# One norm for two and late-turned keys in a second attention's context, and one 96-row product for three in a third expert layer

## The reference

```python
x = x + jnp.tanh(g_xattn[1]) * _L1_xattn_ref(_layernorm(x, axis=-1), ctx_1024, ...)
x = x + jnp.tanh(g_ffn[2]) * _L2_ffn_ref(_layernorm(x, axis=-1), ...)

def _L1_xattn_ref(x, context, Wq, Wkv, Wo, null_kv, q_scale, k_scale, ...):   # 16 heads of 64
    xn = layer_norm(x, ln_in_g, ln_in_b)          # x comes in normalised already: two norms in a row
    cn = layer_norm(context, ln_ctx_g, ln_ctx_b)
    q = xn @ Wq
    k, v = jnp.split(cn @ Wkv, 2, axis=-1)
    ...                                           # a null key and value are appended
    q = l2_normalize(q) * q_scale
    k = l2_normalize(k) * k_scale
    ...

def _L2_ffn_ref(x, gate_W, gate_b, wi_W, wi_b, wo_W, wo_b, lora_A, lora_B):   # E = 8, R = 4, F = 1024
    logits = jnp.einsum('bsd,ed->bse', x, gate_W) + gate_b
    top1 = jnp.argmax(jax.nn.softmax(logits, axis=-1), axis=-1)
    base = jnp.einsum('bsd,fd->bsf', x, wi_W) + wi_b
    for i in range(lora_A.shape[0]):
        lora = jnp.einsum('bsr,fr->bsf', jnp.einsum('bsd,rd->bsr', x, lora_A[i]), lora_B[i])
        inter = jax.nn.relu(base + lora)
        expert_out = jnp.einsum('bsf,df->bsd', inter, wo_W) + wo_b
        out = out + (top1 == i)[..., None] * expert_out
```

## Time and profile before

| | us |
|---|---|
| median of 3 runs | 1950.33 |
| lowest and highest run | 1947.45, 1950.34 |
| profiled execution, whole | 1967.21 |
| profiled execution, span of its trace | 1965.4 |
| TensorE, VectorE, ScalarE, GpSimd busy in the span | 1740.6, 1260.9, 975.3, 529.6 |

### The profile page before, as it was taken

One profiled execution on the slowest core, in us unless ns is written; L12 is line 12 of the kernel. 1 busy time (PEld: TensorE's weight loads), 2 busy tenths in 40 slices (PEclk: granted clock), 3 DMA queues, 4 the chain that ended last, 5 costly groups with the idle time before them and its releaser, 6 DMA issues. The chain is left out here.

```text
span 1965.4 us, 32371 instructions
## 1 busy us (share of the span) xinstructions
PE 1740.6 (89%) x11712; PEld 1417.1 (72%) x11712; DVE 1260.9 (64%) x2310; ACT 975.3 (50%) x1739; POOL 529.6 (27%) x492
## 2 busy tenths in 40 slices
PE   6998799967799997599999969999799789798895
PEld 4666799922577776599999558888577566588884
DVE  6886688545255554688888657765534688666643
ACT  4652466413587763367776234443533255416740
POOL 2220343253323432222221540000200143313333
PEclk9998899978799998699999979999799899999998
DMA  3003478420100000666675230000000200026743
GB/s 112 17 18 98 165 250 255 131 64 0 49 1 7 12 12 25 207 216 237 232 236 203 76 117 1 1 1 1 23 1 1 59 6 17 28 84 207 233 131 94
DMA packets 97139, 178.32 MB, mean 91 GB/s; under 512 B 25184, under 2 KB 61946, under 8 KB 95914
## 3 DMA queue, kind: packets, MB, share of 16 engines
q1 hardware_dynamic: 85496, 146.00, 22.5%
q0 software_dynamic: 11232, 30.69, 5.3%
q10 hardware_dynamic: 288, 0.00, 0.0%
HBM read 149.38 MB, written 27.26 MB: 90 GB/s over the span
## 5 line engine op out<-in xcount | busy, mean ns | idle before, releaser
L1669 POOL DMA_INDIRECT f_block_rows_home<-normed_x,f_token_of_sb x138 | 168.6, 1222 | 425.5 <-PE psum L1715 325.4
L1695 PE MATMUL psum<-f_block_h_sb,f_w1h_home 128*128 128x256 f32 x736 | 211.4, 287 | 30.5 <-DVE f_block_l_sb L1889 11.9
L1695 PE MATMUL psum<-f_block_l_sb,f_w1h_home 128*128 128x256 f32 x736 | 207.0, 281 | 0.0
L1695 PE MATMUL psum<-f_block_h_sb,f_w1l_home 128*128 128x256 f32 x736 | 206.9, 281 | 0.0
L2321 PE MATMUL psum<-a_xT_home,context_w 128*128 128x256 f32 x704 | 181.7, 404 | 13.6 <-PEq L122 9.7
L1705 PE MATMUL psum<-f_w2h_home,f_hidden_h_home 128*128 128x256 f32 x644 | 187.4, 291 | 3.3 <-DVE f_result_sb L1600 2.4
L1705 PE MATMUL psum<-f_w2h_home,f_hidden_l_home 128*128 128x256 f32 x644 | 181.7, 282 | 0.0
L1705 PE MATMUL psum<-f_w2l_home,f_hidden_h_home 128*128 128x256 f32 x644 | 181.7, 282 | 0.0
L1695 PEld LDWEIGHTS psum<-f_block_h_sb,f_w1h_home 128*128 128x128 f32 x736 | 141.0, 192 | 38.5 <-issue 28.6
L2492 ACT ACTIVATE a_probsT_sb<-psum 77x1024 f32<-77x1024 f32 (+1 forms) x128 | 130.8, 1022 | 68.9 <-PE psum L2373 66.3
L2321 PEld LDWEIGHTS psum<-a_xT_home,context_w 128*128 128x128 f32 x704 | 132.1, 197 | 45.1 <-issue 20.0
(11 more groups left out here) (314 smaller groups left out, 3924.1 us busy)
## 6 DMA issues: line engine op xcount, KB each, us to landing
f_w_sb<-in_f_w SPq DMA_DIRECT2D x161, 512.0 KB
sorted_y<-f_result_sb SPq DMA_DIRECT2D x69, 256.0 KB
normed_x<-f_xn_all SPq DMA_DIRECT2D x24, 256.0 KB, 2.1
f_b_row_sb<-in_f_b SPq DMA_DIRECT2D x46, 128.0 KB
f_w_sb<-in_f_w SPq DMA_DIRECT2D x23, 256.0 KB
f_block_rows_home<-normed_x,f_token_of_sb POOLq DMA_INDIRECT x138, 4.3
residual<-in_x SPq DMA_DIRECT2D x8, 256.0 KB, 6.4
context_w<-in_a_wk SPq DMA_DIRECT2D x2, 1024.0 KB, 5.0
```

The lines of the kernel that those rows point to most:

```text
L1669: nc.gpsimd.indirect_dma_start(block_rows[b % 2][:, h, :], None, xs, bass.IndirectOffsetOnAxis(ap=column, axis=0)).then_inc(sems[f"rows_in ...
L1695: last = nc.tensor.matmul(hid_ps(q)[:, m, :], w, rhs, start=(j == 0), stop=(j == len(parts) - 1))
```

## The change

In the context of a1: the two norms in a row are one, with the variance v replaced by v (1 + e) + e^2 (e = 1e-5), so `normalise_once`, `variance_again`, `normalise_again` and the second power go. All 16 value products come first, through four banks; keys are projected one batch a round, and a batch's keys are turned two rounds later; two row tiles are normalised in each of VectorE's rounds and turned two rounds later, through two banks (2 and 3). In the end of f0, `COMBINED` is (5, 11) for (1, 7). In f2: the masked values are written three times beside each other, turned into 96 x 512, and rounded once in place; the second 32 rows then become the rest of u, and the factor `lb`, loaded three times below itself, is rounded, with its third 32 rows made the rest. So `u3` is (uh, ul, uh) and `lb3` is (lbh, lbh, lbl), and one 96-row product gives the three terms. TensorE does the 24 wide products of the first chunk ahead of the turns, and VectorE splits the first weights and inputs within the choice (`beside`).

```diff
@@ rows_part
-        nc.vector.tensor_scalar(var[:, tiles], mv[:, tiles, 1], EPS, None, ALU.add).then_inc(sems["var_done"], 1)
+        if own:
+            last = nc.vector.tensor_scalar(var[:, tiles], mv[:, tiles, 1], 1.0 + EPS, EPS * EPS, ALU.mult, ALU.add)
...
-    def normalise_once(dve, tiles):
-    def variance_again(dve, halves):
-    def normalise_again(dve, tiles):
...
@@ context_part
-    V_BANKS = 1 if own else 4
-    VALUES_FIRST = 10
-    v_bank = lambda j: psum[0:CTX, 6 if own else 4 + j % 4, 0:VN]
+    V_BANKS = 4
+    v_bank = lambda j: psum[0:CTX, (0 if own else 4) + j % 4, 0:VN]
-    key_banks = lambda b: slice(4 * (b % 2), 4 * (b % 2) + 2)
+    key_banks = lambda b: slice(4 + 2 * (b % 2), 6 + 2 * (b % 2))
...
-            if b == 2:
-                rows["power"](pool, 1, slice(0, TILES))
...
-        return range(2 * b - NBATCH, 2 * b - NBATCH + 2) if b >= NBATCH // 2 else range(0)
+        return range(b - 2, b - 1) if 2 <= b < NBATCH else range(NBATCH - 2, NBATCH) if b == NBATCH else range(0)
...
+        for j in range(len(v_list)):
+            value_products(pe, j)
+        for b in range(NBATCH + 2):
+            if b < NBATCH:
+                project(b)
+            for k in rows_beside(b):
+                rows["turn"](pe, k)
+            if b >= 2:
+                turn_keys(b - 2)
...
+        for j in range(len(v_list)):
             own_values_out(j)
+        for b in range(NBATCH + 2):
+            if b < NBATCH:
+                take(b)
+                squares(b)
             for k in rows_beside(b):
                 rows["turned_out"](act, k)
-            spread(b)
+            if b >= 2:
+                spread(b - 2)
...
+        for b in range(NBATCH + 1):
+            if b < NBATCH:
+                sum_squares(b)
+                rows["normalise"](dve, 0, b)
+            if b:
+                normalise_keys(b - 1)
...
@@ choose_low_rank
-        choose.softmax_rows(dve, step, choose.c)
+        choose.shift(dve, step)
+        t["beside"](dve)
+        choose.softmax_rest(dve, step, choose.c)
...
+        nc.vector.tensor_copy(um[:, :, 1:3, :], um[:, :, 0:1, :].to_broadcast([P, TILES, 2, 32])).then_inc(
+            sems["masked"], 1)
...
@@ experts
-        sp.dma_start(lb[:], dram[f"{name}_lb"]).then_inc(sems["lora_in"], 16)
+        for part in range(3):
+            sp.dma_start(lb[part * 32:(part + 1) * 32, :, :], dram[f"{name}_lb"]).then_inc(sems["lora_in"], 16)
...
+        def low_rank(u, c, m):
+            if m == 0 and u == 0:
+                pe.wait_ge(sems["lora_low"], 1)
+                pe.wait_ge(sems["u_low"], c + 1)
+            nc.tensor.matmul(hid_ps[m], lb3[:, u, m * P:(m + 1) * P], u3[:, chunk(c)], start=False,
+                             stop=True).then_inc(sems["hidden"], 1)
+
+        def begin():
+            for m in range(HC):
+                whole_rank(0, 0, m)
+            turn_inputs(0)
+            turn_inputs(1)
+            for m in range(HC):
+                low_rank(0, 0, m)
+            turn_inputs(2)
+            turn_inputs(3)
...
-            nc.scalar.activation(ust[:, k % 2, :], u_ps(k), ACT.Copy)
-            high(uh[:, chunk(k)], u_ps(k), "u_high")
+            high(u3[:, chunk(k)], u_ps(k), "u_high")
         high(w1h[0][:], w1raw[0][:], "w1_high")
+        high(xh[:, :, chunk(0)], xT[:, :, chunk(0)], "x_high")
         t["exponentials"](act)
...
-            low(ul[:, chunk(k)], ust[:, k % 2, :], uh[:, chunk(k)], "u_low")
+            low(u3[32:64, chunk(k)], u_ps(k)[32:64, :], u3[32:64, chunk(k)], "u_low")
...
         dve.wait_ge(sems["lora_high"], 1)
+        low(lb3[64:96], lb[64:96], lb3[64:96], "lora_low")
+        x_low(1)
+        weight_lows(0, 2)
         inputs_low(0)
...
@@ routed_experts
-    COMBINED = (1, 7) if shared == 1 else (4, 12, 20)
+    COMBINED = (5, 11) if shared == 1 else (4, 12, 20)
...
```

More of the change, by code:

```diff
@@ L258, in rows_part @@
     sems = {k: env["sem"](f"{name}r_{k}") for k in (
-        "loaded", "chain", "var_done", "rstd_done", "once", "stats2", "x_normed", "x_turned", "x_out")}
+        "loaded", "chain", "var_done", "rstd_done", "x_normed", "x_turned", "x_out")}
     ln_in = sb("ln_in", [P, 2, DC]) if own else None
@@ L572, in project, with turn_keys @@
             last.then_inc(sems["k_ready"], 1)
[L574 to L585, removed]
+        def turn_keys(b):
             pe.wait_ge(sems["k_normed"], b + 1)
@@ L650, in spread @@
                     keysT[:, part * 4:part * 4 + 4, b, :],
-                    psum[:, 2 + part, 0:4 * keys].rearrange("p (c k) -> p c k", k=keys), ACT.Copy, scale=k_scale[:])
+                    psum[:, part, 0:4 * keys].rearrange("p (c k) -> p c k", k=keys), ACT.Copy, scale=k_scale[:])
             last.then_inc(sems["kn_out"], 1)
[L654 to L657, removed]
+        for j in range(len(v_list)):
             own_values_out(j)
[L659 to L667, removed]
+        for b in range(NBATCH + 2):
+            if b < NBATCH:
+                take(b)
+                squares(b)
             for k in rows_beside(b):
                 rows["turned_out"](act, k)
-            spread(b)
+            if b >= 2:
+                spread(b - 2)
     def scalar(act):
@@ L727, in sum_squares, with normalise_keys @@
             nc.vector.tensor_scalar(ss[b % 3][:], ss[b % 3][:], 1e-24, None, ALU.max).then_inc(sems["squared"], 1)
-        sum_squares(0)
-        sum_squares(1)
-        for b in range(NBATCH):
+        def normalise_keys(b):
             dve.wait_ge(sems["inverted"], b + 1)
@@ L1275, in experts, with run_ahead @@
     y_ps = [psum[:, 4 + q, 0:D] for q in range(4)]
-    u_ps = lambda k: psum[0:32, 4 + k % 2, :]
+    u_ps = lambda k: psum[0:96, 4 + k % 2, :]
     chunk = lambda c: slice(c * CHUNK, (c + 1) * CHUNK)
-    def run_ahead(first, second):
-        first(0, 0)
+    def run_ahead(begin, first, second):
+        begin()
         for u in range(U):
@@ new lines, in whole_rank @@
+        def whole_rank(u, c, m):
+            g = u * CHUNKS + c
+            if m == 0:
+                if c == 0:
+                    pe.wait_ge(sems["w1_low"], u + 1)
+                if u == 0:
+                    pe.wait_ge(sems["x_low"], c + 1)
+            pe.wait_ge(sems["activated"], g * HC + m + 1)
+            cols = slice(m * P, (m + 1) * P)
+            terms = [(w[u][:, k, cols], v[:, k, chunk(c)]) for k in range(DC)
+                     for w, v in ((w1h, xh), (w1h, xl), (w1l, xh))]
+            for j, (w, v) in enumerate(terms):
+                nc.tensor.matmul(hid_ps[m], w, v, start=(j == 0), stop=False)
@@ L1328, in second @@
+        def first(u, c):
+            for m in range(HC):
+                whole_rank(u, c, m)
+                low_rank(u, c, m)
         def second(u, c):
@@ L1342, in second @@
                 last.then_inc(sems["product"], 1)
-        for k in range(CHUNKS):
-            turn_inputs(k)
-        run_ahead(first, second)
+        run_ahead(begin, first, second)
     def scalar(act):
@@ L1435, in vector, with beside @@
         dve.wait_ge(sems["w2_low"], U)
-        run_ahead(first, second)
+        run_ahead(lambda: first(0, 0), first, second)
+    def beside(dve):
+        for wanted, out, whole, part, sem in (("w1_high", w1l[0][:], w1raw[0][:], w1h[0][:], "w1_low"),
+                                              ("x_high", xl[:, :, chunk(0)], xT[:, :, chunk(0)], xh[:, :, chunk(0)],
+                                               "x_low")):
+            dve.wait_ge(sems[wanted], 1)
+            nc.vector.tensor_tensor(out, whole, part.bitcast(F32), ALU.subtract).then_inc(sems[sem], 1)
     def operands_left(engine):
```

101 lines of the change are left out of this document (25 added, 76 removed).

## The result

The changed kernel takes 1894.32 us in the median of four runs (1888.79 to 1896.59); the kernel before took 1948.89 in the same comparison (1945.83 to 1950.34). The ratio is 0.9718, with a 95% interval of 0.9693 to 0.9743: 55 us (50 to 60 by the interval), where 65 had been forecast. The profiled execution of the changed kernel took 1896.59 us, within its runs, and is 70.6 us shorter than the profiled execution before. So the profiles lie 16 us further apart than the runs, and that is what the experiments had to explain.

A forecast was written before the change was run, and what follows sets the result against it. TensorE was taken to bound the third layer, a chain of waits the second attention's context. Savings of 43 (A) and 22 (B) made 65 us: 1950.3 to 1885 us for the median, range 1873 to 1908.

The forecast's parts named there:

- A: Second attention's context, 401 to 520 us: the change was to save 43 to 45 us, taken as 43.
- Value products: Step in the context: ten products sharing one bank become 16 over four banks, 27.6 us, from 401.2 to 428.8.
- pauses and low clock: Among the old value products: ScalarE's 13.8 us wait in two pieces and TensorE at the lower clock, together 16.3 us.
- Rival (1): The context's pauses belong to the profiled execution: A saves 27, the sum is 49, time 1901 us; chance 0.25.
- a releaser without a name: In the context, ScalarE waited 13.8 us in two pieces for a releaser that the profile couldn't name.
- last key copy: End of the context's keys: forecast 74 to 76 us after TensorE's first context product.
- key chain: Context: projection, copy, square, sum, scaling and turning of keys, 4.9 us a batch, with projection 7 ending at 465.1.
- The stall: GpSimd's 4.7 us behind one combine during the context's gathers: it goes, but is worth nothing by itself.
- cover of the four banks: Context values: ScalarE's copy hides under the next product; failing that, 0.9 us more per product, 14 us in all.
- B: Third layer, 1389 to 1527 us: 22 us saved, between 11 and 26, with groups of seven products for nine.
- rival (3): Third layer: 96 rows pay the change of mode, 28 x 0.37 = 10 us less, time 1895 us; chance 0.10.
- The start of the second chunk: Third layer: forecast at 1408.9 to 1410.4, 1.5 to 3 us earlier than before, after a gap of 5 us.

The follow-up runs named there:

- before_again: The kernel before, profiled once more without any edit: median 1942.57 us, ratio 0.9977; second attention's context 104.1 us.
- combined_old: The changed kernel with the combines back at one and seven after the shared blocks, for five and eleven: 1893.81 us, ratio 0.974 to the kernel before.
- vbank1: The changed kernel with one PSUM bank for the value products in place of four: 1909.79 us, ratio 0.9814 to the kernel before.
- B_alone: The kernel before with only the third layer's part of the change, context as before: 1923.47 us, ratio 0.9892.
- one32: The changed kernel with the 96-row low-rank product cut to its first 32 rows: 1911.14 us, ratio 0.9833 to the kernel before.
- one64: The changed kernel with the 96-row low-rank product cut to its first 64 rows: 1906.97 us, ratio 0.9805 to the kernel before.
- late_rounding: The changed kernel with three ScalarE roundings and their VectorE subtractions moved behind the first chunk's activation pairs: 1890.78 us, ratio 0.9721 to the kernel before.
- late_values: The changed kernel with the last three value products moved behind the last projection: 1889.87 us, ratio 0.9715 to the kernel before.
- lag1: The changed kernel with a batch's keys turned one batch later, not two: 1935.12 us, ratio 0.9952 to the kernel before.

## Why the prediction was right or wrong

The direction was right, and the range held the time. The forecast's own span, given as 1874 to 1892, did not; its terms add up to 1875 to 1894, with the result at the edge. The point was 9 us too low. One term was mis-sized, with a smaller one inside it.

*The term that failed is A's 43 us.* The step is the one under *Value products* that puts 16.3 us of pauses and low clock into the length that the change would take away, and then "For the median I subtract the same from 1950.3". before_again, which has neither, puts the pauses and the low clock behind them at 16.4 us. A is 42.4 us between the two profiles (120.5 - 78.1), but 26.0 between executions without pauses (104.1 - 78.1). Rival (1) had 27. The argument against it, "the kernel waits there in any case, for one bank", was the mistake: waiting for the bank costs 0.68 us a product, as the earlier trace rows show at 440.87, not 9. Two signs were in the rows, an excess of 16.9 us over the median and a releaser without a name, and I gave the case a chance of one in four. Without the pauses the prediction's sum is 49 us and its time 1901; that the point missed by 9 us and not by 16 is no merit of the sum.

*Inside A, the handover was missed.* The last key copy ends 73.7 us after the first context product (475.06 - 401.41), just ahead of the 74 to 76 forecast; counted to there, the key chain gains 45.6 us between the profiles. But the next attention starts 4.43 us behind that copy, against 1.28 in before_again, since GpSimd comes 8.01 us after its last power: 3.2 us of the gain are lost in a wait that no step named. 45.6 - 16.4 - 3.2 = 26.0. That this is close to the 26.7 that the forecast has without its pauses (43 - 16.3) is luck in part: the chain gained 2.5 us more than counted, and the handover took 3.2 back.

*The other steps of A held.* The stall was worth nothing (combined_old). The value products took 27.66 us, against 27.6. The cover of the four banks was priced at 14 us and measured at 13.6 (vbank1). From the third batch on, key scalings follow in 4.4 or 5.2 us by turns where I wrote 5.

*B was right*: 22.8 us between the profiles (22 forecast), and in runs 24.6 by the medians of B_alone, 21 by its ratio. A group takes 1.62 us where I took 1.64, because the 96-row product stays with the 128-row ones. one32 and one64 show what rival (3) would have cost: 0.4 us per group. The start of the second chunk was put at 1408.9 to 1410.4, so 19.1 to 20.6 us after the layer's first load; it came at 20.7, after a gap of 4.80 us, and behind it the products ran at the lower clock for 5.3 us (0.77 and 0.63 us each until 1372.5, then 0.40). The Trainium skill (TensorE: Matmul & The Clock Gate, Why this matters for your kernels) warns of idle gaps between bursts; here the trace agrees. In late_rounding the clock fell as well (to 0.51 from 1364 to 1367 us), behind a gap of only 1.97 us.

*What remains.* Stage by stage, A and B make 49 us in undisturbed executions, and the runs 55 (50 to 60). Whether the last 6 are a gain outside the two stretches or the spread of the comparison is not shown; the ratios of the two parts alone add up to some 48.

## What to carry over

A profile is one execution: where its time is above the runs, find the excess in it first, and give nothing for it to the change; a wait whose releaser has no name is the place to look. Products of fewer rows aren't cheaper beside full ones: here joining three factors of 32 rows into one of 96 paid twice, in the count and in the meeting, and 64 rows would not have been enough. And when a chain is shortened, ask for every engine when it reaches the end of the stage, not only for the one that was last.

## What the hardware showed that I hadn't expected

- GpSimd's next instruction stands 8.01 us behind the end of its last power in all eleven kernels that have the new context, though the last key copy ends 3.5 us ahead of it in late_values and 4.5 in lag1. The line that the trace names, L122, is the barrier of all engines in `clear_semaphores`, between the expert layer and the next attention, and TensorE waits there too (5.44 us). Before, GpSimd stood 9.24 us behind its power (before_again), 1.28 us behind the last copy, so that the copies ended last. That the barrier waits for GpSimd is inferred from the constant 8.01; what GpSimd does in that time is not shown.
- A 64-row product among 128-row ones costs as much as a 32-row one (2.03 and 2.02 us a group), while 96 rows cost what 128 do (1.62).
- In late_rounding the clock fell to half within 1.6 us of TensorE taking up work again behind a gap of 1.97 us (one of 1.05 us stands 4 us earlier), and stayed there for 3 us (products of 0.63 us from 1363.69 to 1366.67); behind the changed kernel's gap of 4.80 us it was at half from the first product on.
